# Edge stage of a graph network: spreading the basis rows in four row groups, and placing those copies ahead of a joining

## The reference, cut to what matters

```python
p1 = jnp.tanh(p @ pp_W1 + pp_b1) @ pp_W2 + pp_b2
inter = jnp.concatenate([p1[idx_i], p1[idx_j]], axis=-1)
inter = inter @ pi_W1 + pi_b1
inter = inter @ pi_W2 + pi_b2
inter = (inter @ pi_W3).reshape(inter.shape[0], D, N_BASIS)
i1 = jnp.einsum('ecb,eb->ec', inter, basis)
i1 = jnp.tanh(i1 @ ii_W1 + ii_b1) @ ii_W2 + ii_b2
out = jax.ops.segment_sum(i1, idx_j, num_segments=p1.shape[0])
```

## Time and profile before

| | us |
| --- | --- |
| median of 3 runs | 7844.97 |
| lowest and highest | 7836.37 and 7847.87 |
| the profiled execution's own time | 7882.14 |
| its span | 7880.4 |
| mean granted TensorE clock in it | 0.869 of full speed |
| PE, DVE, ACT, POOL busy in it | 77%, 43%, 17%, 49% |

### The profile page before, as it was taken

One profiled execution on the slowest core, in us unless ns is written; L12 is line 12 of the kernel. 1 busy time (PEld: TensorE's weight loads), 2 busy tenths in 40 slices (PEclk: granted clock), 3 DMA queues, 4 the chain that ended last, 5 costly groups with the idle time before them and its releaser, 6 DMA issues.

```text
span 7880.4 us, 97479 instructions
## 1 busy us (share of the span) xinstructions
PE 6052.0 (77%) x34147; PEld 3017.3 (38%) x34147; DVE 3377.0 (43%) x9846; ACT 1314.6 (17%) x2547; POOL 3857.0 (49%) x4010
## 2 busy tenths in 40 slices
PE   4576777767777677777588888888888889898888
PEld 2233333333333333333244444444444444444444
DVE  7566666666666666666422222233222122234111
ACT  4322223223332232333200000000000000000000
POOL 3244444444444444443266466466466465564564
PEclk9688888888888888888799989899888899898899
DMA  5222223232222222222577677677677678676676
GB/s 167 80 87 90 83 87 89 86 90 83 87 88 87 89 83 87 88 88 84 168 255 245 227 245 248 231 245 241 229 252 241 226 239 268 227 251 233 222 245 197
DMA packets 793158, 1311.95 MB, mean 166 GB/s; under 512 B 235631, under 2 KB 264080, under 8 KB 792160
## 3 DMA queue, kind: packets, MB, share of 16 engines
q1 hardware_dynamic: 574188, 1096.91, 40.6%
q0 software_dynamic: 128032, 186.02, 9.3%
q10 hardware_dynamic: 90452, 22.74, 1.3%
HBM read 1136.21 MB, written 169.12 MB: 166 GB/s over the span
## 4 chain that ended last, share of the span: by engine, by line
PE 41%; issue 7%; another core or an unknown queue 3%; DVE 1%; ACT 0%; DMA 0%; DVEq 0%; ACTq 0%; SPq 0%
PE ps_a L1750 36%; PE ps_w L1778 2%; PE ps_t L1808 1%; PE ps_t L1810 1%; PE ps_t L1812 0%; PE ps_t L1822 0%; PE ps_a L1757 0%; DVE xc L1576 0%; DVE sq L1577 0%; DVE hb L1588 0%; ACT agg L1507 0%; DMA ring<-counts 0%; DVE stat L1574 0%; DVE low L1596 0%
## 5 line engine op out<-in xcount | busy, mean ns | idle before, releaser
L1750 PE MATMUL ps_a<-ring,table 128*128 128x448 fp8e4 x15092 | 3181.4, 366 | 448.5 <-issue 376.0
L1472 POOL DMA_INDIRECT got_rows<-layer_rows,tail_plan x2373 | 2266.0, 955 | 1722.5 <-issue 650.5
L731 POOL DMA_INDIRECT gathered<-u_source,plan x1568 | 1502.8, 958 | 2050.5 <-PE ps_u L944 1498.2
L1750 PEld LDWEIGHTS ps_a<-ring,table 128*128 128x128 f16 x15092 | 1491.9, 101 | 1968.7 <-issue 738.3
L855 DVE TENSOR_TENSOR z<-ps_b,u 128x1024 f32<-128x1024 f32 x784 | 932.0, 1218 | 947.8 <-PE ps_b L955 796.8
L930 PE MATMUL ps_c<-cell_hot,lane_hot 128*128 128x246 f16 x2002 | 436.5, 298 | 951.0 <-ACT unit L758 774.8
L1711 DVE TENSOR_TENSOR tail<-tail,ps_w 128x128 f32 x301 | 86.7, 288 | 2372.3 <-PE ps_w L1778 1230.0
L965 PE MATMUL ps_m<-z,M_sb 128*64 128x512 f32 x3136 | 1057.5, 785 | 0.0
L758 ACT CAST unit<-ps_c 128x490 uint16<-128x490 f32 x924 | 531.3, 575 | 1758.8 <-remote 1222.7
L930 PEld LDWEIGHTS ps_c<-cell_hot,lane_hot 128*128 128x128 f16 x2002 | 153.9, 101 | 1448.1 <-issue 1302.9
L842 DVE TENSOR_SCALAR lane_hot<-iota_n,lane,worth 128x128 f16<-128x128 f16 x2002 | 635.5, 318 | 11.8 <-issue 4.7
(11 more groups left out here) (242 smaller groups left out, 3478.3 us busy)
## 6 DMA issues: line engine op xcount, KB each, us to landing
ring<-counts SPq DMA_DIRECT2D x308, 1792.0 KB
ring<-counts SPq DMA_DIRECT2D x154, 1904.0 KB
counts<-unit SPq DMA_DIRECT2D x154, 784.0 KB
dst_all<-targets_in_ring SPq DMA_DIRECT2D x196, 256.0 KB
got_rows<-layer_rows,tail_plan POOLq DMA_INDIRECT x2373
gathered<-u_source,plan POOLq DMA_INDIRECT x1568
layer_rows<-table ACTq DMA_DIRECT2D x84, 224.0 KB
window<-u_target SPq DMA_DIRECT2D x392, 32.0 KB
```

The source lines that it names most:

```text
L731: pool.indirect_dma_start(gathered[q][:, i, :], None, Us, bass.IndirectOffsetOnAxis(ap=T["plan"][:, at:at + 1], axis=0)).then_inc(S[f"rows ...
L1472: pool.indirect_dma_start(got_rows[s][:, i, :], None, G["tables"][n % 2], bass.IndirectOffsetOnAxis(ap=T["tail_plan"][:, at:at + 1], axis= ...
L1750: last = mm(ps_a[:, b, 0:BC].rearrange("p (u c) -> p u c", u=BU), table[n % 2][:, k, :], cells, start=(k == 0), stop=(k == TILES - 1 and n ...
```

## The change

1. The basis of a group is loaded four times, by four DMAs, to partitions 0, 32, 64 and 96 onward (16 rows each). `sel` gets its ones in the rows of the matching 32-row block, by another constant in `prepare`. Each of the four matmuls of S0 and S1 reads only its own 32 rows of both operands. The count that PE waits for on `bas` is four times as large.
2. On PE, J0 of the next group moves behind S1 and C2: J0 S1 C2 J1 becomes S1 C2 J0 J1.

```diff
@@ prepare, DVE
             for i in range(4):
                 for h in range(2):
-                    nc.vector.memset(which[:, i, h, :], float(2 * i + h))
+                    nc.vector.memset(which[:, i, h, :], float((32 + 2) * i + h))
@@ edges, SP
                 def load_basis(g):
-                    sp.dma_start(basis16[g % 2][0:2 * NB, :], B16[:, g * EG:(g + 1) * EG]).then_inc(S[f"bas{g % 2}"], 16)
+                    for i in range(4):
+                        sp.dma_start(basis16[g % 2][32 * i:32 * i + 2 * NB, :], B16[:, g * EG:(g + 1) * EG]).then_inc(S[f"bas{g % 2}"], 16)
@@ edges, PE
                 def spread(g, h):
 
                     q, s = g % 2, 2 * g + h
-                    pe.wait_ge(S[f"bas{q}"], 16 * (g // 2 + 1))
+                    pe.wait_ge(S[f"bas{q}"], 64 * (g // 2 + 1))
                     for p in range(2):
                         if s:
                             pe.wait_ge(S["z_done"], 2 * s + p - 1)
                         for i in range(2 * p, 2 * p + 2):
-                            last = mm(ps_b[:, i, :], T["sel"][:, i, :], basis16[q][:, HG * h:HG * h + HG], start=True, stop=True)
+                            rows = slice(32 * i, 32 * i + 32)
+                            last = mm(ps_b[:, i, :], T["sel"][rows, i, :], basis16[q][rows, HG * h:HG * h + HG], start=True, stop=True)
                         last.then_inc(S["b_done"], 1)
@@ edges, PE, the order of an iteration
-                    if g < LAST:
-                        join(g + 1, 0)
                     spread(g, 1)
                     for k in counts[2:3]:
                         count(k)
+                    if g < LAST:
+                        join(g + 1, 0)
                     if g < LAST:
                         join(g + 1, 1)
```

## The result

| | before | after |
| --- | --- | --- |
| median, us | 7840.67 (4 runs) | 8034.96 (4 runs, 8032.48 to 8036.77) |
| ratio | | 1.0247, 95% interval 1.023 to 1.0265 |
| span of the profiled execution, us | 7880.4 | 8030.8 |
| mean granted TensorE clock in it | 0.869 | 0.843 |

The changed kernel is slower by 194 us in the medians. Between the two profiled executions it is 150 us, because that of before (7882) lies 41 us above the median of its runs. The first gather of the last group moved from 3696 to 3865 us, so 169 us are in the edge stage; the rest of the two traces differs by 18 us the other way.

The account below looks back on a forecast made before the run. The prediction took a loop of waits in the edge stage, held by POOL's gathers, as the bound. J0 later by 0.65 us in 194 groups adds 126 us to the median of 7845: 7970, eight-in-ten range 7710 to 8110.

Parts of the forecast that it names:

- the mechanism: Edge stage: J0 comes later while the time from first gather to ACT's release stays unchanged; 7970 us, chance 0.56.
- the forecast of 126 us: Edge stage: J0 later by a mean of 0.65 us in each of 194 groups with gathers behind them.
- The loop of waits: Edge stage: no engine is full, so a loop of waits sets the pace, 17.5 us a group.
- the release: ACT's emptying of a count after its long wait for "remote", some 11.6 us after a group's first gather.
- S1 and C2 on the path: PE, ahead of J0: the two steps delay J0 by 0.54 us at full clock, 0.94 at half.
- the change of shape: PE: 0.1 us a group added for changing the array's shape, estimated from P3 and L965.
- no side by side: Rival on PE: S1's four matmuls serialize, J0 later by a mean of 1.6 us; +310 us, 8155; chance 0.12.
- What leaves the shadow: PE's work between first gather and release, 11.6 us that it does not shorten: taking work out gains nothing.
- the edge: Last prompt emptying, 3.44 us after the first gather; if C5 came before it, 7717 us; signals-early rival's chance 0.23.
- Three loads, SP, `prepare`: Three extra basis DMAs cost SP 1.0 to 2.0 us more, covered by slack; changed constants in `prepare` cost nothing.
- Z: DVE, second half: can start earlier since S1 is ahead of J0; worth 0, as DVE has idle time around it.

Follow-up runs that it names:

- half_gathers: The kernel before with four gathers a group instead of eight, half of the source rows left out; 6510.3 us in one run.
- direct_rows: The kernel before with POOL's eight indirect gathers a group replaced by eight plain loads of fixed rows issued by SP; 6642.27 us in one run.
- s1_ahead: The changed kernel with C2 put back behind J0 (S1 J0 C2 J1); 7919.35 us, 1.0120 of before.
- after_s1_rows: The changed kernel with S0 reading all 128 rows again, S1 still in row groups ahead of J0; 8027.28 us, 1.0249 of before.
- order_only: The kernel before with only the new order on PE (S1 C2 J0 J1), no row groups; 7984.34 us, 1.0198 of before.
- rows_only: The changed kernel with the old order on PE (J0 S1 C2 J1), keeping row groups and four basis loads; 7733.92 us, 0.9878 of before.
- s1_rows: Old order on PE and four basis loads, with only S1 in row groups, against the kernel before; 7705.27 us, 0.9838.
- s0_rows: Old order on PE and four basis loads, with only S0 in row groups, against the kernel before; 7888.93 us beside 7881.97, 1.0014.
- early_j0: The changed kernel with J0 moved behind P0 and its copy on ACT behind the first emptied count; 7033.30 us, 0.8976 of before.

## Why the prediction was right, and where it was not

The direction, the mechanism and the range of 7710 to 8110 held; the forecast of 126 us was 68 short of the measured 194. The narrower 7920 to 8030, given for this mechanism by itself, was missed by 5 us: one term was left out, the clock.

- **The loop of waits, and where the period is fixed: right.** From the first gather to the release it is 11.63 us before and 11.59 after. half_gathers and direct_rows show that it hangs on POOL's indirect gathers, which the prediction took from the end of the stage.
- **S1 and C2 on the path: right.** The forecast was 0.54 at full clock (0.215, 0.22, and 0.1 for the change of shape) and 0.94 at half clock; the earlier trace rows and the rows after give 0.32 + 0.12 to 0.22, and 0.55 + 0.38. The mean is 0.44 + 0.27 = 0.71 where 0.65 was taken. The four matmuls run at once, and the rival "no side by side" is gone. The 0.1 us was rightly sized, but not where it was put. From P3's start to S1's it is 2234.09 - 2232.18 = 1.91 at half clock, and to J0's in the kernel before (rows below) 2007.48 - 2005.57 = 1.91 as well; in stretches wholly at full clock it is 1.01 in both (medians of 17 and 53 groups). The extra time lies between S1's start and C2's: 0.32 where one matmul is 0.215. The Trainium skill (TensorE: Matmul & The Clock Gate, Part 3: Packing small matmuls) has 3.07 times for such a packing. The trace gives 1.71 / 0.55 = 3.1 at half clock, which agrees, and 0.86 / 0.32 = 2.7 at full clock, which is less.

PE of the kernel before, a group at half clock, in its timeline:

```profile
2005.57 1.98 PE L965 MATMUL ps_m<-z,M_sb 128*64 128x512 f32 x4
2007.48 0.61 PE L940 MATMUL ps_u<-from_node,window 128*128 128x512 f16 x1
```

- **The clock: the term that was missing.** The sum let all other steps between release and gather keep their durations. They took 0.26 us more a group: +0.16 up to P3, +0.10 from P3 on, at a granted clock of 0.58 instead of 0.61, in a stage at 0.79 instead of 0.84 (0.84 stands in the earlier trace rows). 0.26 x 194 = 50 us, and 0.06 x 194 = 12 us for the mean of S1 and C2: 126 + 50 + 12 = 188. That the medians give 194 is in part luck, as the traces themselves are 169 apart. s1_ahead shows the same from the other side, 0.51 us back for a step of 0.27.

That the 0.26 is the clock can be read step by step. The 0.10 from P3 on: at a given level the stretch is equally long in both kernels (1.01 and 1.91), but it ran wholly at full clock in 53 of 168 groups before and in 17 of the changed kernel. The 0.16 up to P3 lies in the groups of six (4.88 us before, 5.19 in the changed kernel). Where PE was at the lower level nearly all the way from the release to P3 (48 of them before, 71 changed), C1 starts 4.83 us after the release in both, and P3 at 5.15 and at 5.35 (medians); in nearly all others the clock rose earlier still. C1 of two such groups, the first from the kernel before with P3 behind it at 2025.71, the second from the changed kernel with P3 at 2253.54:

```profile
2025.39 0.39 PE L930 MATMUL ps_c<-cell_hot,lane_hot 128*128 128x246 f16 x2
...
2253.02 0.59 PE L931 MATMUL ps_c<-cell_hot,lane_hot 128*128 128x246 f16 x2
```

C1 takes 0.32 in the one, at a granted clock of 0.92, and 0.52 in the other, at 0.50: the clock rises at C1 before, and only behind it in the changed kernel. P3 is at 5.35 also in after_s1_rows, so the shorter S0 is not the cause, and at 5.15 in order_only and in s1_ahead. So neither the order alone nor the row groups with C2 behind J0 bring it about. Why the clock rises later in the changed kernel is open.

- **What leaves the shadow is worth nothing: right for this kernel, wrong as a rule.** In the old order the same row groups in S1 gained 1.2 to 1.6%, by releases that come at about 8.3 or 9.8 us after the first gather. The prediction expected C5 about 1 us earlier, near 4.3 us after the first gather, and put the edge before which its signal would pass at 3.44. That did not come: in the changed kernel C5 is over at 5.31 us on average, before at 5.20. Nor is the moment of C5 what decides. It is 4.48 in order_only, 4.69 in rows_only, 4.80 in s1_ahead and 4.84 in s1_rows, with 24, 29, 4 and 28 early releases, and counts that were over at 4.55 in before were held to the end all the same. What decides is open.
- **Three loads, SP, `prepare`: right** as far as seen; with the row groups of S0 they come to 1.0014 (s0_rows).
- **Z:** nothing speaks against its 0, and DVE's waits moved as forecast, but no run tests it alone.

Read as two edits, the change is one that gains 1.2% in the order that it found (rows_only), and a new order that costs 2.0% alone (order_only) and turns the other's gain into a small loss: 1.0247 / 0.9878 is 3.7% for the order in the company of row groups. A forecast by the sum of the parts cannot show that.

## What to carry to other kernels

Before a step is made shorter, find the one that the slow engine's next start waits for: what stands in front of it costs its duration and a share again through its neighbours' clock, and what stands behind it may be worth nothing. Where an engine idles because a signal is held, put the work that starts the next round there; J0 behind P0 gained 10.2%, and the row groups beside it nothing. Bringing more forward than that can lose (3 to 7% here), so try the steps one by one.

## What the runs showed of the hardware that I had not expected

- While POOL issues indirect DMAs one behind another (0.95 us each, 0.30 apart), what PE signals late in the row reaches ACT 5 to 7 us after the matmul is over, in most groups 2.5 to 3 us after the start of the last gather. With four gathers in place of eight, or eight plain loads from SP, it is not so (periods of 10.80 and 11.27 us against 17.59). Counts that are over within 3.3 us of the first gather (groups of five, before) are emptied at 3.46 on average, so without such a delay. The cause within the chip is not shown.
- Now and then a held signal passes earlier, at 8.3 or about 10 us. Row groups in S1 alone moved the number of such groups of six from 2 in 84 to 28 in 84, and the kernel is 1.6% faster.
- Four 32-row matmuls of 512 columns run at an overlap of 3.9 by the modelled records. S1 then takes 0.32 us in place of 0.86 at full clock. In front of them no delay is seen (1.01 us from P3's start either way); some 0.1 us more than one matmul lies between them and the next full-size one.
- s1_rows beats both kernels with a line changed (0.9838), and early_j0 by far (0.8976).
